# Graph network on one core: the update stage's two normalisations move from VectorE to ScalarE

## The chip, the cores and the metric

The kernel runs on one core of one Trainium2 chip. A core has TensorE (PE, with its weight loads shown as PEld), VectorE (DVE), ScalarE (ACT), GpSimd (POOL) and the queues that start transfers, SyncE's (SP) among them. The metric is the device time of one execution in microseconds; lower is better. Each engine works through its own instructions in order; semaphores connect them.

## The reference, cut to what matters

Two graph layers over 12500 nodes of 256 features and 200000 edges, each followed by a layer norm. What matters here is what is done for each node between the two edge passes:

```python
msgs = jnp.where(deg[:, None, None] > 0, agg, V)          # agg is already summed over the edges
out = msgs.reshape(N, H * D) @ Wo + bo
y = out + node_features
z = (y - mean(y)) / sqrt(var(y) + 1e-05) * gamma + beta   # end of the first layer
x1 = _layernorm(x + z)                                    # (v - m) / sqrt(var + eps)
x0_i = leaky(x1 @ W1 + b1);  x0_j = leaky(x1 @ W2 + b2)   # leaky(v) = max(v, 0.2 v)
a1 = x0_i @ wa1 + ba1[0];    a2 = x0_j @ wa2 + ba2[0]     # used by the second edge pass
```

All of it is float32.

## The kernel before

The kernel has seven stages in a row: projections of all nodes, a sort of the edges' keys beside the edge scores, the softmax, the aggregation over edges, `update_nodes` (the update stage, the node work shown above), `attend` (the second edge pass) and `finish`. Each stage is a block of its own, and the change is in `update_nodes` alone.

The nodes lie in NB = 98 blocks of 128, one node on each partition. `update_nodes` is a software pipeline written out by hand: every engine runs a loop over turns i, and in a turn it does each of its steps for the block i - lag, in the order in which the steps stand in a list. A block goes through these steps:

- DVE `divide` (lag 0) and `fill_alone` (0) make msg: the sum divided by the softmax's denominator, and V for nodes without edges. Both read two tensors in SBUF. PE `turn_msg` (0) transposes msg, ACT `copy_msg_t` (0) copies it out of PSUM, PE `project_msg` (1) multiplies by Wo.
- DVE `add_x` (2) makes y from PSUM and x. DVE `y_spread` and `y_variance` (2), ACT `root_y` (2), DVE `invert_y` (3) make mean and 1/std in columns of the tile `small`. DVE `normalise_y` (3) is line 1288: (y - mean) * (1/std), in place.
- POOL multiplies by gamma (line 1130), adds beta (1132), adds x (1134), which gives z. The first of these waits for `y_normed`.
- DVE `z_spread` and `z_variance` (5), ACT `root_z` (5), DVE `invert_z` (6), DVE `normalise_z` (6), line 1283, make x1 from z. The tiles msg, y, z and x1 have four buffers each.
- PE `turn_x1` (7) and ACT `copy_x1_t` (7) transpose x1, ACT `double` (7) writes 2 * x1 into the table of nodes, PE `project_x1` (8) multiplies by W1 and W2 at once, ACT `fifth` (8) writes 0.2 times the result, DVE `leak` (9) takes the maximum, and DVE `row_sum1` and `row_sum2` (9) make the two dot products, each with two inputs in SBUF. SP stores the rows of the block (lag 12).

In the trace the msg, y, z and x1 tiles are all called `score`, since they share that tensor's space; CUSTOM_DVE_ANT_0 is the dot product of row_sum1 (L1236) and row_sum2 (L1275), with a short reading of the accumulator behind it; BATCH_NORM_STATS2 is a spread, BATCH_NORM_AGGREGATE a variance.

DVE's order within a turn is the list in its loop: leak, add_x, z_spread, divide, row_sum1, invert_z, invert_y, y_spread, z_variance, row_sum2, normalise_z, normalise_y, y_variance, fill_alone. ACT's is fifth, copy_x1_t, root_z, double, root_y, copy_msg_t. PE's is project_x1, turn_x1, project_msg, turn_msg.

Of the kernel before, what the change touches and what calls it, by code (L numbers as in the profile page):

```python
# [7 lines left out]
ALU = mybir.AluOpType  # L8
ACT = mybir.ActivationFunctionType
# [1023 lines left out]
def update_nodes(nc, t, wo, bo, gamma, beta, w1, b1, w2, b2, wa1, ba1, wa2, ba2):  # L1033

    with ExitStack() as ctx:
# [3 lines left out]
        def ring(name, shape, n=4):  # L1039
            return [sb(f"{name}{u}", shape) for u in range(n)]  # L1040
# [4 lines left out]
        def sem(name):  # L1045
            return ctx.enter_context(nc.semaphore(name))
# [11 lines left out]
        msg, y, z, x1 = ([t["score"][:, (4 * k + u) * D:(4 * k + u + 1) * D] for u in range(4)] for k in range(4))  # L1058
        msg_t, x1_t = ring("n_msg_t", [P, 2, P]), ring("n_x1_t", [P, 2, P])
        hx, small = ring("n_hx", [P, D + XW]), ring("n_small", [P, 24], 8)  # L1060
# [7 lines left out]
        y_var, y_over, y_normed, z_stats, z_var = (sem(f"n_{n}") for n in ("y_var", "y_over", "y_normed", "z_stats", "z_var"))  # L1068
        z_over, x1_ready, a1_ready, xj_ready = (sem(f"n_{n}") for n in ("z_over", "x1_ready", "a1_ready", "xj_ready"))
        msg_t_ready, y_std, z_std, doubled, x1_t_ready, leaked = (sem(f"n_{n}") for n in ("msg_t_ready", "y_std", "z_std", "doubled", "x1_t_ready", "leaked"))  # L1070
        fifth_ready = sem("n_fifth_ready")
        msg_turned, o_ready, x1_turned, h_ready = (sem(f"n_{n}") for n in ("msg_turned", "o_ready", "x1_turned", "h_ready"))
        z_scaled, z_moved, z_ready = sem("n_z_scaled"), sem("n_z_moved"), sem("n_z_ready")
        block = ctx.enter_context(nc.Block())
# [61 lines left out]
        @block.scalar  # L1136
        def _(act):
            act.wait_ge(pads_set, 5)

            def fifth(b):  # L1140
                act.wait_ge(h_ready, b + 1)
                if b >= 4:
                    act.wait_ge(xj_ready, b - 3)
                    act.wait_ge(xj_stored[b % 4], 16 * (b // 4))
                nc.scalar.activation(hx[b % 4][:, 0:2 * D], ps_h[b % 2][:, :], ACT.Copy, scale=0.2).then_inc(fifth_ready, 1)

            def copy_x1_t(b):
                act.wait_ge(x1_turned, b + 1)
                if b >= 4:
                    act.wait_ge(h_ready, b - 3)  # L1150
                nc.scalar.copy(x1_t[b % 4][:, :, :], ps_x1[b % 2][:, :, :]).then_inc(x1_t_ready, 1)

            def root_z(b):
                act.wait_ge(z_var, b + 1)
                nc.scalar.activation(small[b % 8][:, 18:19], small[b % 8][:, 15:16], ACT.Sqrt, bias=eps[:, 0:1]).then_inc(z_std, 1)

            def double(b):
                act.wait_ge(x1_ready, b + 1)
                nc.scalar.activation(tab[:, b * AW:b * AW + D], x1[b % 4], ACT.Copy, scale=2.0).then_inc(doubled, 1)

            def root_y(b):
                act.wait_ge(y_var, b + 1)
                nc.scalar.activation(small[b % 8][:, 16:17], small[b % 8][:, 13:14], ACT.Sqrt, bias=eps[:, 0:1]).then_inc(y_std, 1)

            def copy_msg_t(b):
                act.wait_ge(msg_turned, b + 1)
                if b >= 4:
                    act.wait_ge(o_ready, b - 3)
                nc.scalar.copy(msg_t[b % 4][:, :, :], ps_msg[b % 2][:, :, :]).then_inc(msg_t_ready, 1)

            for i in range(NB + 9):
                for lag, work in ((8, fifth), (7, copy_x1_t), (5, root_z), (7, double), (2, root_y), (0, copy_msg_t)):
                    if live(i - lag):
                        work(i - lag)

# [42 lines left out]
        @block.vector  # L1218
        def _(dve):
            den = slots[:, :, D:AW]  # L1220
            dve.tensor_scalar(alone[:, :].unsqueeze(2), den[:, :, 0:1], 0.0, None, ALU.is_equal).then_inc(over_ready, 1)
            dve.tensor_scalar(over[:, :, :], den, 0.5, None, ALU.max).then_inc(over_ready, 1)
            dve.wait_ge(over_ready, 2)
            dve.reciprocal(over[:, :, :], over[:, :, :]).then_inc(over_ready, 1)
            dve.wait_ge(over_ready, 3)
            dve.wait_ge(weights_in, 12 * 16)
            dve.wait_ge(pads_set, 5)

            def leak(b):
                dve.wait_ge(fifth_ready, b + 1)  # L1230
                dve.tensor_tensor(hx[b % 4][:, 0:2 * D], ps_h[b % 2][:, :], hx[b % 4][:, 0:2 * D], ALU.max).then_inc(leaked, 1)

            def row_sum1(b):
                dve.wait_ge(leaked, b + 1)
                h = hx[b % 4]
                dve.tensor_tensor_reduce(h[:, 0:D], h[:, 0:D], wide["wa1"][:, :], 1.0, 0.0, ALU.mult, ALU.add, t["a1_tab"][:, b:b + 1])\  # L1236
                    .then_inc(a1_ready, 1)

            def add_x(b):
                dve.wait_ge(o_ready, b + 1)  # L1240
                dve.wait_ge(x_loaded[b % X_RING], 16 * (b // X_RING + 1))
                if b >= 4:
                    dve.wait_ge(z_ready, b - 3)
                dve.tensor_tensor(y[b % 4], ps_o[b % 2][:, :], x_in[b % X_RING][:, :], ALU.add).then_inc(y_ready, 1)

            def z_spread(b):
                dve.wait_ge(z_ready, b + 1)
                dve.bn_stats(small[b % 8][:, 6:12], z[b % 4]).then_inc(z_stats, 1)

            def divide(b):  # L1250
                if b >= 4:
                    dve.wait_ge(msg_turned, b - 3)
                dve.tensor_tensor(msg[b % 4].rearrange("p (h d) -> p h d", h=H), tab[:, b * AW:b * AW + D].rearrange("p (h d) -> p h d", h=H),
                                  over[:, b, :].unsqueeze(2).broadcast_to([P, H, DH]), ALU.mult).then_inc(divided, 1)

            def invert_z(b):
                dve.wait_ge(z_std, b + 1)
                dve.reciprocal(small[b % 8][:, 19:20], small[b % 8][:, 18:19]).then_inc(z_over, 1)

            def invert_y(b):  # L1260
                dve.wait_ge(y_std, b + 1)
                dve.reciprocal(small[b % 8][:, 17:18], small[b % 8][:, 16:17]).then_inc(y_over, 1)

            def y_spread(b):
                dve.wait_ge(y_ready, b + 1)
                dve.bn_stats(small[b % 8][:, 0:6], y[b % 4]).then_inc(y_stats, 1)

            def z_variance(b):
                dve.wait_ge(z_stats, b + 1)
                dve.bn_aggr(small[b % 8][:, 14:16], small[b % 8][:, 6:12]).then_inc(z_var, 1)  # L1270

            def row_sum2(b):
                dve.wait_ge(a1_ready, b + 1)
                h = hx[b % 4]
                dve.tensor_tensor_reduce(h[:, 0:D], h[:, D:2 * D], wide["wa2"][:, :], 1.0, 0.0, ALU.mult, ALU.add, h[:, 2 * D:2 * D + 1])\  # L1275
                    .then_inc(xj_ready, 1)

            def normalise_z(b):
                dve.wait_ge(z_over, b + 1)
                if b >= 4:  # L1280
                    dve.wait_ge(x1_turned, b - 3)
                    dve.wait_ge(doubled, b - 3)
                dve.tensor_scalar(x1[b % 4], z[b % 4], small[b % 8][:, 14:15], small[b % 8][:, 19:20], ALU.subtract, ALU.mult)\
                    .then_inc(x1_ready, 1)

            def normalise_y(b):
                dve.wait_ge(y_over, b + 1)
                dve.tensor_scalar(y[b % 4], y[b % 4], small[b % 8][:, 12:13], small[b % 8][:, 17:18], ALU.subtract, ALU.mult)\
                    .then_inc(y_normed, 1)

            def y_variance(b):
                dve.wait_ge(y_stats, b + 1)
                dve.bn_aggr(small[b % 8][:, 12:14], small[b % 8][:, 0:6]).then_inc(y_var, 1)

            def fill_alone(b):
                dve.wait_ge(divided, b + 1)
                dve.wait_ge(v_loaded[b % 4], 16 * (b // 4 + 1))
                dve.scalar_tensor_tensor(msg[b % 4], v_in[b % 4][:, :], alone[:, b:b + 1], msg[b % 4], ALU.mult, ALU.add).then_inc(msg_ready, 1)

            for i in range(NB + 10):  # L1300
                for lag, work in ((9, leak), (2, add_x), (5, z_spread), (0, divide), (9, row_sum1), (6, invert_z), (3, invert_y), (2, y_spread),
                                  (5, z_variance), (9, row_sum2), (6, normalise_z), (3, normalise_y), (2, y_variance), (0, fill_alone)):
                    if live(i - lag):
                        work(i - lag)
            dve.wait_ge(a1_ready, NB)
            dve.tensor_scalar(t["a1_tab"][:, :], t["a1_tab"][:, :], ba[:, 0:1], ba[:, 1:2], ALU.add, ALU.add)
            dve.wait_ge(xj_ready, NB)
# [224 lines left out]
```

## Time and profile before

| | |
|---|---|
| median of 3 runs | 7487.49 us (7469.43 to 7493.04) |
| the profiled execution | 7541.05 us, of which the span of the trace is 7539.4 |
| the update stage's full turns in it | 4561.6 to 4963.6 us after the span's start |
| busy share of the whole span | PE 71%, DVE 60%, POOL 55%, ACT 41% |

The shares of the whole span are averages over stages with different limits, so the stage itself has to be read by windows. Times in the rows are microseconds from the span's start unless marked ns. A row of the timeline gives start, length, engine, line and operation; a bracket at its end is idle time of the engine before it and what ended it.

### The profile page before, as it was taken

How to read it: one execution, taken by the hardware profiler on the slowest of the kernel's cores; microseconds unless marked ns; L12 is line 12 of the kernel's file. 1: busy time of each engine (PE TensorE's matmuls, PEld its weight loads, DVE VectorE, ACT ScalarE, POOL GpSimd, SP SyncE). 2: the span in 40 equal slices, each digit the busy share in tenths (PEclk: the TensorE clock that was granted, in tenths of full speed). 3: DMA queues.
4: the chain of work that ended last, by engine and by line, in shares of the span. 5: the costliest groups of instructions: out<-in, count | busy, mean ns of one | idle time of the engine just before them, and what ended most of it. 6: DMA issues, size and time to landing. Idle time of an engine off the chain costs nothing. (4 is left out here: it accounts for less than half of the span.)

```text
span 7539.4 us, 82733 instructions
## 1 busy us (share of the span) xinstructions
PE 5366.9 (71%) x21563; PEld 4019.8 (53%) x21563; DVE 4547.7 (60%) x8352; ACT 3080.2 (41%) x8260; POOL 4117.2 (55%) x4183
## 2 busy tenths in 40 slices
PE   5966666666667556637777768877777777777874
PEld 2445555555555444425555544446666666666663
DVE  6216666767677555578888878964444444444446
ACT  2323333333333333328777754433333333333333
POOL 1126666666667555513333325556666666666663
PEclk9976776767666676669999999987777777777776
DMA  2348888888898888816666643323333333333333
GB/s 74 106 146 281 276 292 285 276 287 289 291 299 290 287 280 275 274 36 199 199 199 199 199 142 88 88 78 92 91 91 91 91 91 91 91 91 91 91 92 112
DMA packets 857534, 1308.71 MB, mean 174 GB/s; under 512 B 87145, under 2 KB 690535, under 8 KB 856787
## 3 DMA queue, kind: packets, MB, share of 16 engines
q0 software_dynamic: 221008, 683.55, 29.1%
q1 hardware_dynamic: 629091, 613.77, 26.1%
q10 hardware_dynamic: 7010, 6.38, 0.2%
q8 instruction: 187, 3.06, 0.2%
q14 instruction: 238, 1.95, 0.1%
HBM read 1031.10 MB, written 272.26 MB: 173 GB/s over the span
## 5 line engine op out<-in xcount | busy, mean ns | idle before, releaser
L645 POOL DMA_INDIRECT s_rows<-kv_rows,other x1664 | 1737.3, 1044 | 949.3 <-issue 496.1
L1340 POOL DMA_INDIRECT t_rows<-xj_rows,other x1664 | 1626.0, 977 | 837.5 <-issue 444.6
L1415 PE MATMUL ps_xsum<-t_rows,t_hot_att 128*128 128x256 f32 x3328 | 1235.7, 536 | 417.5 <-DVE node_tab L1386 388.7
L754 PE MATMUL ps_rel<-rel,hot 64*128 64x64 f32 x3328 | 613.0, 341 | 862.6 <-DVE s_rows L737 628.5
L756 PE MATMUL ps_q<-node_tab,hot 128*128 x3328 | 1191.6, 518 | 36.1 <-issue 35.6
L1415 PEld LDWEIGHTS ps_xsum<-t_rows,t_hot_att 128*128 128x128 f32 x3328 | 863.8, 272 | 594.6 <-issue 356.1
L754 PEld LDWEIGHTS ps_rel<-rel,hot 64*128 64x128 f32 x3328 | 552.3, 249 | 1057.2 <-issue 969.3
L734 DVE TENSOR_TENSOR s_rows<-s_rows,ps_rel 128x1024 f32<-128x1024 f32 x416 | 506.4, 1217 | 931.8 <-remote 706.7
L661 ACT ACTIVATE hot<-apart,ones 128x1024 f32<-128x1024 bf16 x416 | 477.8, 1148 | 1373.3 <-remote 767.7
L1027 PE MATMUL ps_sum<-a_terms,a_hot 128*128 128x260 f32 x3328 | 830.1, 392 | 282.7 <-DVE node_tab L1006 193.3
L756 PEld LDWEIGHTS ps_q<-node_tab,hot 128*128 128x128 f32 x3328 | 817.3, 258 | 221.0 <-issue 42.6
L987 ACT ACTIVATE a_terms<-a_terms,score 128x64 f32<-128x64 f32 x3328 | 839.8, 334 | 218.8 <-DMA a_terms<-v_edges 218.1
L1386 DVE TENSOR_TENSOR node_tab<-node_tab,ps_xsum 128x256 f32 x1664 | 699.9, 421 | 363.1 <-issue 181.1
L1027 PEld LDWEIGHTS ps_sum<-a_terms,a_hot 128*128 128x128 f32 x3328 | 599.3, 190 | 513.3 <-issue 430.2
L1006 DVE TENSOR_TENSOR node_tab<-node_tab,ps_sum 128x260 f32 x1664 | 703.5, 423 | 183.0 <-DVE node_tab L1006 5.4
L972 POOL TENSOR_TENSOR a_terms<-a_terms,score 128x512 f32<-128x512 f32 x416 | 438.2, 1053 | 661.6 <-DMA a_terms<-v_edges 661.6
L1377 DVE TENSOR_TENSOR t_logit<-ps_a,t_rows 128x4 f32<-128x4 f32 x416 | 67.4, 162 | 1084.0 <-DMA x_in<-in_x 1036.4
L1360 ACT COPY t_node_hot<-ps_hot 128x512 f32<-128x512 f32 x416 | 243.8, 586 | 915.9 <-remote 831.9
L656 ACT ACTIVATE apart<-apart,minus_p 128x1024 bf16<-128x1024 bf16 x416 | 473.4, 1138 | 326.6 <-DMA apart<-what_rows 239.4
L1353 ACT ACTIVATE t_hot_att<-t_hot,t_att 128x128 f32<-128x128 f32 x1664 | 531.6, 390 | 13.6
L737 DVE TENSOR_TENSOR s_rows<-s_rows,ps_q 128x1024 f32<-128x1024 f32 x416 | 507.8, 1221 | 14.2
L739 DVE TENSOR_REDUCE score<-s_rows 128x16 f32<-128x1024 f32 x416 | 507.4, 1220 | 14.2
(208 smaller groups left out, 5835.0 us busy)
## 6 DMA issues: line engine op xcount, KB each, us to landing
v_edges<-s_rows SPq DMA_DIRECT2D x416, 512.0 KB
a_terms<-v_edges SPq DMA_DIRECT2D x416, 512.0 KB, 3.7
apart<-what_rows SPq DMA_DIRECT2D x416, 256.0 KB
s_rows<-kv_rows,other POOLq DMA_INDIRECT x1664
t_rows<-xj_rows,other POOLq DMA_INDIRECT x1664
kv_rows<-kv_out POOLq DMA_DIRECT2D x97, 256.0 KB, 2.3
xj_rows<-n_hx SPq DMA_DIRECT2D x97, 130.0 KB, 2.1
x_in<-in_x SPq DMA_DIRECT2D x97, 128.0 KB, 2.0
```

The lines of the kernel that those rows point to most:

```text
L645: pool.indirect_dma_start(out=rows[g % KV_RING][:, k, :], out_offset=None, in_=t["kv_rows"], in_offset=bass.IndirectOffsetOnAxis(ap=t["oth ...
L737: dve.tensor_tensor(key, key, ps_q[g % 2][:, :, :], ALU.mult).then_inc(picked_used, 1)
L739: dve.tensor_reduce(t["score"][:, g * U * H:(g + 1) * U * H].rearrange("p (k h) -> p k h", h=H), by_head, AX.X, ALU.add)\
L754: nc.tensor.matmul(ps_rel[g % 2][:, k, :], hot[g % 2][0:R, 1, k, :], rel_02[:, :], start=True, stop=True)
L756: last = nc.tensor.matmul(ps_q[g % 2][:, k, :], hot[g % 2][:, 0, k, :], t["node_tab"][:, bass.ds(blocks[k] * AW, D)], start=True, stop=True)
L987: last = nc.scalar.activation(head, head, ACT.Copy, scale=t["score"][:, at:at + 1])
L1006: dve.tensor_tensor(acc, acc, ps_sum[g % 2][:, k, 0:AW], ALU.add).then_inc(added, 1)
L1027: last = nc.tensor.matmul(ps_sum[g % 2][:, k, 0:AW], hot[g % 4][:, k, :], terms[g % DEEP][:, k, :], start=True, stop=True)
L1340: pool.indirect_dma_start(out=rows[g % RING][:, k, :], out_offset=None, in_=t["xj_rows"], in_offset=bass.IndirectOffsetOnAxis(ap=t["other1 ...
L1353: last = nc.scalar.activation(hot_att[g % 2][:, k, :], hot[g % 4][:, k, :], ACT.Copy, scale=att[g % 2][:, k:k + 1])
L1386: dve.tensor_tensor(acc, acc, ps_sum[g % 2][:, k, :], ALU.add).then_inc(added, 1)
L1415: last = nc.tensor.matmul(ps_sum[g % 2][:, k, :], hot_att[g % 2][:, k, :], rows[g % RING][:, k, 0:D], start=True, stop=True)
```

## The change

DVE no longer normalises. Behind each reciprocal it makes one more column, the shift -mean * (1/std): `shift_z` into column 21 of `small`, `shift_y` into column 20. ACT then computes x * (1/std) + shift with one Identity activation, which takes the scale from one column and the bias from the other: `normalise_z` (lag 6) and `normalise_y` (lag 3) stand at the end of ACT's turn. The waits of normalise_z for the buffer of x1 (`x1_turned`, `doubled`) go along with it. In DVE's turn the two reciprocals move from behind row_sum1 to behind add_x, and the shifts stand behind row_sum1. Lags, buffers and the other engines' orders stay.

```diff
# ScalarE
+            def normalise_z(b):
+                act.wait_ge(z_shift, b + 1)
+                if b >= 4:
+                    act.wait_ge(x1_turned, b - 3)
+                    act.wait_ge(doubled, b - 3)
+                nc.scalar.activation(x1[b % 4], z[b % 4], ACT.Identity, scale=small[b % 8][:, 19:20], bias=small[b % 8][:, 21:22])\
+                    .then_inc(x1_ready, 1)
+
+            def normalise_y(b):
+                act.wait_ge(y_shift, b + 1)
+                nc.scalar.activation(y[b % 4], y[b % 4], ACT.Identity, scale=small[b % 8][:, 17:18], bias=small[b % 8][:, 20:21])\
+                    .then_inc(y_normed, 1)
+
             for i in range(NB + 9):
-                for lag, work in ((8, fifth), (7, copy_x1_t), (5, root_z), (7, double), (2, root_y), (0, copy_msg_t)):
+                for lag, work in ((8, fifth), (7, copy_x1_t), (5, root_z), (7, double), (2, root_y), (0, copy_msg_t),
+                                  (6, normalise_z), (3, normalise_y)):
...
# VectorE
-            def normalise_z(b):
+            def shift_z(b):
                 dve.wait_ge(z_over, b + 1)
-                if b >= 4:
-                    dve.wait_ge(x1_turned, b - 3)
-                    dve.wait_ge(doubled, b - 3)
-                dve.tensor_scalar(x1[b % 4], z[b % 4], small[b % 8][:, 14:15], small[b % 8][:, 19:20], ALU.subtract, ALU.mult)\
-                    .then_inc(x1_ready, 1)
-
-            def normalise_y(b):
+                dve.tensor_scalar(small[b % 8][:, 21:22], small[b % 8][:, 14:15], small[b % 8][:, 19:20], -1.0, ALU.mult, ALU.mult)\
+                    .then_inc(z_shift, 1)
+
+            def shift_y(b):
                 dve.wait_ge(y_over, b + 1)
-                dve.tensor_scalar(y[b % 4], y[b % 4], small[b % 8][:, 12:13], small[b % 8][:, 17:18], ALU.subtract, ALU.mult)\
-                    .then_inc(y_normed, 1)
+                dve.tensor_scalar(small[b % 8][:, 20:21], small[b % 8][:, 12:13], small[b % 8][:, 17:18], -1.0, ALU.mult, ALU.mult)\
+                    .then_inc(y_shift, 1)
...
             for i in range(NB + 10):
-                for lag, work in ((9, leak), (2, add_x), (5, z_spread), (0, divide), (9, row_sum1), (6, invert_z), (3, invert_y), (2, y_spread),
-                                  (5, z_variance), (9, row_sum2), (6, normalise_z), (3, normalise_y), (2, y_variance), (0, fill_alone)):
+                for lag, work in ((9, leak), (2, add_x), (6, invert_z), (3, invert_y), (5, z_spread), (0, divide), (9, row_sum1), (6, shift_z),
+                                  (3, shift_y), (2, y_spread), (5, z_variance), (9, row_sum2), (2, y_variance), (0, fill_alone)):
```

## Rows read from the trace of the kernel before

**Rows 1.** Windows: stretch, its length, busy PE, PEld, DVE, ACT, POOL; clock, DMA.

```profile
4700.00:4800.00 100.00, 86.74 (x312) 41.69 (x310) 100.00 (x356) 45.08 (x136) 53.29 (x66) 1.00 0.32 88
```

**Rows 2.** Timeline, DVE: the leaks of turn 9 and turn 98.

```profile
4561.59 0.69 DVE L1231 TENSOR_TENSOR n_hx<-ps_h,n_hx 128x512 f32<-128x512 f32 x1 [1.10 <-ACT n_hx L1145]
...
4963.57 0.68 DVE L1231 TENSOR_TENSOR n_hx<-ps_h,n_hx 128x512 f32<-128x512 f32 x1
```

**Rows 3.** Timeline, DVE: one steady turn, from leak to the next leak.

```profile
4701.36 0.68 DVE L1231 TENSOR_TENSOR n_hx<-ps_h,n_hx 128x512 f32<-128x512 f32 x1
...
4701.96 0.41 DVE L1244 TENSOR_TENSOR score<-ps_o,n_x 128x256 f32<-128x256 f32 x1
...
4702.62 0.50 DVE L1253 TENSOR_TENSOR score<-node_tab,n_over 128x256 f32<-128x256 f32 x1
...
4703.04 0.94 DVE L1236 CUSTOM_DVE_ANT_0 n_hx<-n_hx,wide_wa 128x256 f32<-128x256 f32 x1
...
4703.92 0.15 DVE L1258 RECIPROCAL n_small<-n_small 128x1 f32<-128x1 f32 x1
...
4704.05 0.40 DVE L1266 BATCH_NORM_STATS2 n_small<-score 128x6 f32<-128x256 f32 x1
...
4704.46 0.39 DVE L1275 CUSTOM_DVE_ANT_0 n_hx<-n_hx,wide_wa 128x256 f32<-128x256 f32 x1
...
4704.78 0.40 DVE L1283 TENSOR_SCALAR score<-score,n_small 128x256 f32<-128x256 f32 x1
...
4705.10 0.40 DVE L1288 TENSOR_SCALAR score<-score,n_small 128x256 f32<-128x256 f32 x1
...
4705.43 0.17 DVE L1293 BATCH_NORM_AGGREGATE n_small<-n_small 128x2 f32<-128x6 f32 x1
4705.52 0.45 DVE L1298 SCALAR_TENSOR_TENSOR score<-n_v,n_alone,score 128x256 f32<-128x256 f32 x1
...
4705.89 0.68 DVE L1231 TENSOR_TENSOR n_hx<-ps_h,n_hx 128x512 f32<-128x512 f32 x1
```

**Rows 4.** Timeline, DVE: row_sum1 of turn 9.

```profile
4563.41 0.42 DVE L1236 CUSTOM_DVE_ANT_0 n_hx<-n_hx,wide_wa 128x256 f32<-128x256 f32 x1
```

**Rows 5.** Timeline, POOL: its three operations about that steady turn.

```profile
4702.11 0.74 POOL L1132 TENSOR_TENSOR score<-score,wide_beta 128x256 f32<-128x256 f32 x1
...
4702.92 0.79 POOL L1134 TENSOR_TENSOR score<-score,n_x 128x256 f32<-128x256 f32 x1
...
4705.65 0.91 POOL L1130 TENSOR_TENSOR score<-score,wide_gamma 128x256 f32<-128x256 f32 x1 [1.94 <-DVE score L1288]
```

**Rows 6.** Timeline, PE: turn_msg at both ends of a turn without waits.

```profile
4562.30 0.44 PE L1210 MATMUL ps_msg<-ident,score 128*128 128x128 f32 x2
...
4566.15 0.44 PE L1210 MATMUL ps_msg<-ident,score 128*128 128x128 f32 x2
```

**Rows 7.** Timeline, ACT: copy_msg_t, fifth and copy_x1_t of the steady turn.

```profile
4701.97 0.37 ACT L1169 COPY n_msg_t<-ps_msg 128x256 f32<-128x256 f32 x1 [0.57 <-PE ps_msg L1210]
...
4704.00 0.60 ACT L1145 ACTIVATE n_hx<-ps_h 128x512 f32<-128x512 f32 x1 [1.66 <-PE ps_h L1187]
...
4704.50 0.37 ACT L1151 COPY n_x_t<-ps_x 128x256 f32<-128x256 f32 x1
```

**Rows 8.** Groups of ACT, whole span: busy us, mean ns, idle before.

```profile
L1353 ACT ACTIVATE t_hot_att<-t_hot,t_att 128x128 f32<-128x128 f32 x1664 | 531.6, 390 | 13.6
L310 ACT ACTIVATE enh<-ps_xt,q 128x128 f32<-128x128 f32 x196 | 61.8, 376 | 7.4 <-PE ps_xt L339 7.4
...
L1159 ACT ACTIVATE node_tab<-score 128x256 f32<-128x256 f32 x98 | 40.6, 415 | 0.0
...
L1163 ACT ACT_TABLE_LOAD x1 | 1.3, 1283 | 0.0
```

**Rows 9.** Line L371 (ns min/median/max), and POOL's timeline beside it.

```profile
L371 DVE TENSOR_SCALAR pbit<-pid x7: 153/154/154, 72.1 to 73.2; 128x1 int32<-128x1 int32 x7
...
72.28 0.42 POOL L102 TENSOR_TENSOR b_rest<-b_qkv,b_part 6x128 f32<-6x128 f32 x1
```

More of the change, by code:

```diff
@@ L1070, in update_nodes @@
         msg_t_ready, y_std, z_std, doubled, x1_t_ready, leaked = (sem(f"n_{n}") for n in ("msg_t_ready", "y_std", "z_std", "doubled", "x1_t_ready", "leaked"))
-        fifth_ready = sem("n_fifth_ready")
+        fifth_ready, y_shift, z_shift = sem("n_fifth_ready"), sem("n_y_shift"), sem("n_z_shift")
         msg_turned, o_ready, x1_turned, h_ready = (sem(f"n_{n}") for n in ("msg_turned", "o_ready", "x1_turned", "h_ready"))
```

## The prediction, made before the changed kernel was run

> **What bounds the kernel now.** I read the windows by stage first. From turn 9 of the update stage on, DVE is busy for all 100.00 us of a 100 us window, PE for 86.74 at full clock, ACT for 45.08, POOL for 53.29 [rows 1]. So in the full turns the stage runs at DVE's pace: whatever leaves DVE's queue shortens the turn, until another engine takes over. Next I read the timeline for the two leaks that bound the 89 full turns (block 97's last DVE work included): (4963.57 - 4561.59) / 89 = 4.517 us a turn [rows 2]. Then one turn of DVE, start by start [rows 3]. The reader is to see in it that the displayed lengths overlap by about 0.08 us (fill_alone ends at 4705.97, leak starts at 4705.89), so that a cost is the distance between starts; and that one operation is out of line. row_sum1 lasts 0.94 us; the same operation took 0.42 in turn 9, when POOL was idle [rows 4]. In the steady turn it starts at 4703.04, while POOL's last addition runs from 4702.92 to 4703.71 [rows 5]. Likewise `divide` takes 0.50 beside POOL's second operation. The pairs fit an exclusive hold: a DVE operation that reads two tensors in SBUF waits until about 0.14 us before the end of a POOL operation that started first (4703.98 - 0.42 = 4703.56 beside an end at 4703.71; 4703.12 less the 0.41 that add_x takes for the same shape = 4702.71, beside an end at 4702.85), and a POOL operation that meets a DVE one is stretched: 0.91 in place of the 0.74 of the second, so that it gets its inputs as if it had asked for them 0.14 to 0.15 after its start (4705.97 - 4705.65 - 0.17) [rows 3, 5]. leak and add_x have one input in PSUM and stand beside POOL unharmed. So where POOL's three operations lie in DVE's turn is worth 0.6 us now, and the change moves them.
>
> **The edit, DVE.** Out go the two 128x256 normalisations: y_variance starts 0.65 us after normalise_z [rows 3]. In come two products on one column, shift_z and shift_y. The nearest row is `reciprocal` on a column, 0.15 long, with 0.13 for the pair start to start [rows 3]; a 128x1 TENSOR_SCALAR with constants is 0.154 long [rows 9]. A scalar read from SBUF may add as much as a column costs, so the pair lies between 0.13 and 0.26; I take 0.26, the dearer end, since both read a column as their scalar. Moving the reciprocals changes no sum. Free of POOL, the turn is 4.53 - 0.65 + 0.26 - 0.52 (row_sum1) - 0.09 (divide) = 3.53.
>
> **ACT** gets two 128x256 passes. Nothing here has scale and bias columns together. Below: L1159's plain pass, 0.415 [rows 8]. With a scale column, 128 columns of L1353 take 0.390; the slope between 512 and 256 columns, (0.60 - 0.37) / 256, adds 0.115: 0.50 [rows 7, 8]. L310's bias column costs 0.12 over 0.37 - 0.115, which gives at most 0.62. Start to start is 0.10 less (L1145 is 0.60 long, its successor starts after 0.50 [rows 7]): 0.32, 0.40, 0.52. I take 0.40 to 0.52; ACT's busy time then goes from 2.04 us a turn (0.4508 x 4.52) to 2.9 to 3.1, so it isn't the bound, and its old duties are ahead of the passes in its queue.
>
> **Where the passes lie decides.** normalise_z and normalise_y stand behind copy_msg_t, which waits for fill_alone and PE's transposes of the same turn. With F the end of fill_alone as zero, copy_msg_t starts at 0.53 (4701.97 against 4701.44) [rows 3, 7], the passes at 0.80 and 1.20 to 1.32, the second ends at 1.70 to 1.94, and POOL starts 0.15 later, as it does behind normalise_y today (4705.10 + 0.40, 4705.65) [rows 3, 5]: p = 1.85 to 2.09. Today it starts 0.32 before F. What waits for it, z_spread, comes two turns later; what waits for x1_ready (at 1.42 at the latest) is turn_x1, which PE reaches only behind project_x1, whose end starts fifth at 4704.00, 2.56 after F [rows 7]. Both are covered. PE's queue is not reordered, nor SP's; SP waits for z_ready only six blocks back and for msg_ready four.
>
> **The new turn**, with the distances of [rows 3] (add_x and z_spread are 0.66 together, y_spread to row_sum2 is 0.41), from F: leak -0.08, add_x 0.52, invert_z 0.85, invert_y 0.92, z_spread 0.98, divide 1.31 (no POOL beside it now), row_sum1 1.64, that is before p. It ends at 2.06; POOL's first operation is stretched to max(p, 1.92) + 0.73 = 2.65 to 2.82. DVE: shift_z 1.98, shift_y 2.11, y_spread 2.24, row_sum2 at 2.65 (0.41 on), held up by 0 to 0.03, ends 3.04. POOL's second wants to start at 2.73 to 2.90 and is held by row_sum2, ends at 3.04 - 0.14 + 0.73 = 3.63. y_variance 2.97, fill_alone 3.06: it meets POOL's second, gets the inputs at 3.49, ends at **3.94 to 3.98; I take 3.95**. So the 0.6 of waiting for POOL doesn't vanish: it moves from row_sum1 to fill_alone and is 0.43 there. POOL's third ends about 0.6 after F, clear of divide.
>
> **PE's floor.** Between 4562.30 and 4566.15 PE waited for nothing: 3.85 us a turn [rows 6]. So PE is nearly the bound; P can't be under 3.85 in full turns.
>
> **Sum.** 89 x (4.517 - 3.95) = 50.5 us. In the nine turns ahead of these DVE waits for the others (1.10 us before turn 9's leak [rows 2]), and in the nine behind them project_x1 and the work behind it remain; y_normed half a turn later costs them nothing, or up to the 2 us by which it is late; I take 0. Against the profiled execution (7539.4 us of span, 7541.05 in all) that is 7490.5; on the median of the runs, 7487.49, which is 0.7% below it, 7437. The stage ran at full clock in the profile and the edit touches no other, so the difference carries over in us, not in per cent.
>
> [...] In the rows of a steady turn no TENSOR_SCALAR meets POOL. Seven on one column, back to back from 72.1 to 73.2, all took 153 to 154 ns, though POOL ran a TENSOR_TENSOR from 72.28 to 72.70 among them [rows 9]: a column isn't held up. [...]
>
> **Rivals.** Faster by over 0.3% means over 22.5 us, or 0.25 us a turn; within that a measurement can't tell it from no change.
> (a) The shifts are held by POOL's first operation, which waits behind row_sum1 and goes ahead of them: shift_z at 2.51 instead of 1.98, row_sum2 then 3.18, held by POOL's second (which waited for shift_y) to 3.31, fill_alone 3.72 held by the third to 4.15, F at 4.60. 89 x 0.08 = +8: 7495. [...] Against it: the 153 ns rows. 7 in 100.
> (b) POOL comes first: p below 1.64, so that row_sum1 waits as it does today. It needs ACT's passes at the plain 0.415 (p = 0.80 + 0.32 + 0.42 + 0.15 = 1.69) and 0.05 more. Then row_sum1 gets its inputs at 2.2, row_sum2 runs 3.19 to 3.58, POOL's third is held by it and ends at 4.17, fill_alone waits to 4.03: F at 4.49, 7485, no change. The margin is small, but both column rows say the passes are dearer. 8 in 100.
> (c) Slower: the table of ACT's functions. A table load is 1.28 us [rows 8]. If Identity and Sqrt didn't share one, every turn would have two loads: ACT's starts sum to about 2.5 + 2.57 = 5.07 us, 89 x 0.55 = +49: 7536. It decides from 2.0 us more on ACT in a turn; one load would not. Against it: Copy and Sqrt already alternate under the single load of L1163, and Identity and Copy under the first one. 3 in 100.
> (d) An undrawn wait (POOL later than 2.1, or a lost slot of ACT) puts the turn at 4.1 to 4.4: 7450 to 7477. For it: p is the least certain of my terms, and from p = 2.05 on every 0.1 costs 0.1. 13 in 100, most of it still faster by over 0.3%.
>
> **Numbers.** My forecast, P from 3.85 to 4.05, has 68 in 100: 7428 to 7446, and with the spread of the runs 7422 to 7455. For 8 in 10 I add (d) and most of (b): 7422 to 7485. Faster: 0.68 and 0.10 of (d), 0.78. Same: (a), (b), the rest of (d), 0.18. Slower: (c) and what I have not thought of, 0.04.
>
> **What would show it.** After: full turns of 3.95 us; PE over 0.95 busy; row_sum1 near 0.42 and fill_alone near 0.88; POOL's first operation starting 1.85 to 2.09 after fill_alone's end, ended by ACT; no column shift over 0.25 us; ACT passes of 0.50 to 0.62; one table load in the stage. Wrong if row_sum1 is still 0.9 long (b), if the shifts are 0.5 long (a), if table loads stand in the turns (c).

## The result and the profile after

The changed kernel takes 7440.25 us in the median of 6 runs (7426.93 to 7447.64) against 7487.02 for the kernel before, also 6 runs: a ratio of 0.9936, with a 95% interval from 0.9924 to 0.9947. The forecast was 7437 in a range of 7422 to 7485.

The windows of the changed kernel, with the columns of [rows 1]:

```profile
4700.00:4800.00 100.00, 100.00 (x358) 48.08 (x357) 100.00 (x412) 74.06 (x205) 58.50 (x77) 1.00 0.38 102
```

In [rows 1] only DVE was busy throughout. Now PE's row shows 100.00 as well (its ends are modelled, so waits of 0.1 us vanish in it), ACT's share rose from 45 to 74, and the clock stayed at full. The two leaks that bound the 89 full turns, from the timeline:

```profile
4531.33 0.69 DVE L1245 TENSOR_TENSOR n_hx<-ps_h,n_hx 128x512 f32<-128x512 f32 x1 [1.30 <-ACT n_hx L1145]
...
4879.69 0.68 DVE L1245 TENSOR_TENSOR n_hx<-ps_h,n_hx 128x512 f32<-128x512 f32 x1
```

That is (4879.69 - 4531.33) / 89 = 3.914 us a turn against 4.517 in [rows 2], so 53.6 us less in the full turns. Turn 9, the first of them, took 4.48 us (4.13 before); the other 88 took 3.908 on average, against 4.521. The rest of the stage kept its length: from the first divide to the first leak 34.4 us (33.9 before), from leak 98 to the last row_sum2 27.6 (27.6). The span fell by more, 7539.4 to 7444.0, but 31 of those us lie ahead of the stage and 11 behind it, where nothing was edited. The profiled execution of the kernel before, 7541.05 us, lies outside its six runs (7469.43 to 7498.27), so these two spans can't be set against each other. That is why the stage is read by itself and the whole by medians.

One turn of the timeline answers to [rows 3], [rows 5] and [rows 7]. It begins with fill_alone, whose end, 4703.09 + 0.85 = 4703.94, is the zero of the prediction's positions:

```profile
4703.09 0.85 DVE L1309 SCALAR_TENSOR_TENSOR score<-n_v,n_alone,score 128x256 f32<-128x256 f32 x1
...
4704.46 0.37 ACT L1169 COPY n_msg_t<-ps_msg 128x256 f32<-128x256 f32 x1 [0.33 <-PE ps_msg L1224]
...
4704.73 0.60 ACT L1176 ACTIVATE score<-score,n_small 128x256 f32<-128x256 f32 x1
...
4705.23 0.59 ACT L1181 ACTIVATE score<-score,n_small 128x256 f32<-128x256 f32 x1
4705.24 0.40 DVE L1267 TENSOR_TENSOR score<-node_tab,n_over 128x256 f32<-128x256 f32 x1
...
4705.57 0.41 DVE L1250 CUSTOM_DVE_ANT_0 n_hx<-n_hx,wide_wa 128x256 f32<-128x256 f32 x1
...
4705.91 0.20 DVE L1294 TENSOR_SCALAR n_small<-n_small 128x1 f32<-128x1 f32 x1
4705.97 0.72 POOL L1130 TENSOR_TENSOR score<-score,wide_gamma 128x256 f32<-128x256 f32 x1 [1.45 <-ACT score L1181]
4706.04 0.20 DVE L1299 TENSOR_SCALAR n_small<-n_small 128x1 f32<-128x1 f32 x1
...
4706.57 0.40 DVE L1289 CUSTOM_DVE_ANT_0 n_hx<-n_hx,wide_wa 128x256 f32<-128x256 f32 x1
4706.77 0.79 POOL L1132 TENSOR_TENSOR score<-score,wide_beta 128x256 f32<-128x256 f32 x1
...
4707.00 0.84 DVE L1309 SCALAR_TENSOR_TENSOR score<-n_v,n_alone,score 128x256 f32<-128x256 f32 x1
```

The reader is to see four things. The second pass ends at 4705.82 and POOL starts 2.03 us after fill_alone's end, released by ACT (in [rows 5] by DVE, 0.32 before it). row_sum1 is 0.41 long, not 0.94. fill_alone is 0.84 long, not 0.45: it starts at 4707.00, inside POOL's second operation (4706.77 to 4707.56). And shift_y runs from 4706.04 to 4706.24 beside POOL's first operation without a stretch of either.

### The profile page after: what moved, and what is told of

The parts are those of the page before. It is cut to its first block and busy times, and to the rows that moved or that the text cites. A ratio compares the mean times of both kernels' runs of the same rounds, so it can differ in the third digit from the quotient of the medians.

```text
span 7444.0 us, 82929 instructions
## 1 busy us (share of the span) xinstructions
PE 5245.8 (70%) x21563; PEld 3935.2 (53%) x21563; DVE 4486.9 (60%) x8352; ACT 3169.2 (43%) x8456; POOL 4088.2 (55%) x4183
## 3 DMA queue, kind: packets, MB, share of 16 engines
q8 instruction: 187, 3.06, 0.2%
q14 instruction: 240, 1.97, 0.1%
## 5 line engine op out<-in xcount | busy, mean ns | idle before, releaser
L1426 PE MATMUL ps_xsum<-t_rows,t_hot_att 128*128 128x256 f32 x3328 | 1184.7, 519 | 484.3 <-DVE node_tab L1397 449.1
L756 PE MATMUL ps_q<-node_tab,hot 128*128 x3328 | 1168.3, 509 | 53.1 <-issue 52.4
L754 PE MATMUL ps_rel<-rel,hot 64*128 64x64 f32 x3328 | 597.9, 335 | 855.4 <-DVE s_rows L737 615.5
L1426 PEld LDWEIGHTS ps_xsum<-t_rows,t_hot_att 128*128 128x128 f32 x3328 | 832.3, 262 | 648.2 <-issue 439.3
L756 PEld LDWEIGHTS ps_q<-node_tab,hot 128*128 128x128 f32 x3328 | 800.8, 252 | 234.9 <-issue 64.9
```

The lines of the kernel that those rows point to most:

```text
L754: nc.tensor.matmul(ps_rel[g % 2][:, k, :], hot[g % 2][0:R, 1, k, :], rel_02[:, :], start=True, stop=True)
L756: last = nc.tensor.matmul(ps_q[g % 2][:, k, :], hot[g % 2][:, 0, k, :], t["node_tab"][:, bass.ds(blocks[k] * AW, D)], start=True, stop=True)
L1426: last = nc.tensor.matmul(ps_sum[g % 2][:, k, :], hot_att[g % 2][:, k, :], rows[g % RING][:, k, 0:D], start=True, stop=True)
```

## The experiments

Two theories go through all of them. **Queue:** only what leaves or enters DVE's queue counts, since DVE is the bound. **Holding:** a DVE operation with two inputs in SBUF, or a 256-column TENSOR_SCALAR, and a POOL operation shut each other out, the first to start going first, so that the positions of both count. The second part rests on normalise_z in y_only, below. The turn of each kernel is read as above, from two leaks 89 turns apart:

| kernel | leaks of turn 9 and turn 98 | full turn, us | expected (holding) | median, us | ratio, 95% interval |
|---|---|---|---|---|---|
| before | 4561.59, 4963.57 | 4.517 | | 7487.02 | 1 |
| changed | 4531.33, 4879.69 | 3.914 | 3.95 | 7440.25 | 0.9936 (0.9924 to 0.9947) |
| order_only | 4552.27, 4942.91 | 4.389 | 4.43 | 7532.67 | 0.9992 (0.9982 to 1.0002) |
| passes_old_order | 4547.20, 4895.81 | 3.917 | 3.91 | 7485.90 | 0.9927 (0.9911 to 0.9944) |
| y_only | 4542.02, 4956.99 | 4.663 | 4.57 to 4.75 | 7552.26 | 1.0018 (1.0006 to 1.0029) |
| z_only | 4557.97, 4960.61 | 4.524 | 4.49 | 7541.72 | 1.0005 (0.9995 to 1.0015) |
| passes_before_copy | 4527.86, 4925.87 | 4.472 | 4.04 | 7484.29 | 0.9995 (0.9983 to 1.0007) |
| y_after_fifth | 4512.26, 4857.82 | 3.883 | 3.85 | 7432.74 | 0.9933 (0.9918 to 0.9948) |
| before_no_beta | 4527.75, 4883.21 | 3.994 | 3.98 | 7452.85 (one run) | |
| after_no_beta | 4522.55, 4871.23 | 3.918 | 3.91 | 7433.23 (one run) | |
| after_again | 4072.65, 4421.01 | 3.914 | 3.91 | 6632.60 | 0.9928 (0.9914 to 0.9941) |
| four_apart | 4071.51, 4414.51 | 3.854 | 3.85 | 6628.96 | 0.9916 (0.9902 to 0.9930) |
| four_apart_no_b12 | 4077.03, 4401.44 | 3.645 | 3.65 | 6610.05 (one run) | |

The groups ran on three different chips, so a median is only to be set against the kernel before of its own group: 7536.75 us for the first four experiments, 7487.18 for the next four, 6683.89 for the last three. The ratios do that.

**order_only: the order alone.**

```diff
-(9, leak), (2, add_x), (5, z_spread), (0, divide), (9, row_sum1), (6, invert_z), (3, invert_y), (2, y_spread), ...
+(9, leak), (2, add_x), (6, invert_z), (3, invert_y), (5, z_spread), (0, divide), (9, row_sum1), (2, y_spread), ...
```

> The kernel before with only invert_z and invert_y moved from behind row_sum1 to behind add_x. Two theories. Holding: a DVE operation with two SBUF inputs waits for a POOL operation that started first, so the place of each against POOL's three counts. Divide then starts 1.31 us after fill_alone's end instead of 1.18, when POOL's second operation has let go (about 1.27), and is no longer held (0.41 long, not 0.49); row_sum1 still is (about 0.95). Full turn 4.43 us against 4.52, so 8 us less: about 7479. Queue: only what leaves or enters DVE's queue counts, so 4.52 and no change.

Most turns are 4.43 us long; nine of 4.03 bring the mean to 4.389. DVE's queue has the same operations in it, so the 0.09 of a typical turn came from where divide lies. By the line's own rows, min/median/max in ns:

```profile
L1253 DVE TENSOR_TENSOR score<-node_tab,n_over x98: 395/401/930, 4518.5 to 4939.9; 128x256 f32<-128x256 f32 x98
...
L1236 DVE CUSTOM_DVE_ANT_0 n_hx<-n_hx,wide_wa x98: 399/942/947, 4554.2 to 4970.1; 128x256 f32<-128x256 f32 x98
```

divide's median fell from 0.49 to 0.40, row_sum1's is still 0.94. The 11 us that the stage lost are at the edge of what the whole-kernel ratio can tell (0.9982 to 1.0002).

The turns of 4.03 were not expected. In them row_sum1 went ahead of POOL's third operation, which had started 0.17 before it, and in the next turn POOL went first with the same lead:

```profile
4633.32 1.16 POOL L1134 TENSOR_TENSOR score<-score,n_x 128x256 f32<-128x256 f32 x1
4633.49 0.41 DVE L1236 CUSTOM_DVE_ANT_0 n_hx<-n_hx,wide_wa 128x256 f32<-128x256 f32 x1
...
4637.35 0.82 POOL L1134 TENSOR_TENSOR score<-score,n_x 128x256 f32<-128x256 f32 x1
4637.52 0.94 DVE L1236 CUSTOM_DVE_ANT_0 n_hx<-n_hx,wide_wa 128x256 f32<-128x256 f32 x1
```

So the first to start does not always go first.

**passes_old_order: the move alone.**

```diff
-... (2, add_x), (6, invert_z), (3, invert_y), (5, z_spread), (0, divide), (9, row_sum1), (6, shift_z), (3, shift_y), (2, y_spread), (5, z_variance), (9, row_sum2), ...
+... (2, add_x), (5, z_spread), (0, divide), (9, row_sum1), (6, invert_z), (3, invert_y), (2, y_spread), (5, z_variance), (9, row_sum2), (6, shift_z), (3, shift_y), ...
```

> Both passes on ACT as in the changed kernel, but DVE's order as before (reciprocals behind row_sum1, shifts where the normalisations were). Holding: row_sum1 starts 1.51 after fill_alone's end and is free, row_sum2 comes to 2.39, inside POOL's first operation (2.03 to 2.76), waits until about 2.61; fill_alone then gets its inputs at about 3.46: full turn 3.91 us, as in the changed kernel (3.91 measured), with the waiting split between row_sum2 (0.62 long) and fill_alone (about 0.63). The new order is worth nothing: 7440. A theory that gives the order a share of the gain expects 4.0 or more.

```profile
L1289 DVE CUSTOM_DVE_ANT_0 n_hx<-n_hx,wide_wa x98: 389/644/916, 4550.0 to 4923.5; 128x256 f32<-128x256 f32 x98
...
L1309 DVE SCALAR_TENSOR_TENSOR score<-n_v,n_alone,score x98: 452/601/740, 4513.8 to 4895.3; 128x256 f32<-128x256 f32 x98
```

The waiting is split as expected, 0.24 at row_sum2 and 0.16 at fill_alone instead of 0.40 at fill_alone, and the turn is the same. With both passes on ACT, the new order is worth nothing.

**y_only and z_only: one pass each.** The other normalisation goes back to DVE, in the place of its shift.

```diff
# y_only, DVE: normalise_z as before, in the place of shift_z; ACT:
-                                  (6, normalise_z), (3, normalise_y)):
+                                  (3, normalise_y)):
# z_only, DVE: normalise_y as before, in the place of shift_y; ACT:
-                                  (6, normalise_z), (3, normalise_y)):
+                                  (6, normalise_z)):
```

> Only normalise_y on ACT; normalise_z stays on DVE, in the place of shift_z. Queue: about half of the gain, a turn of 4.1 to 4.2 us, 7460. Holding: without normalise_z ahead of it, normalise_y ends 0.5 us earlier and POOL starts 1.54 after fill_alone's end instead of 2.03, beside row_sum1 (1.64). Then normalise_z is held by POOL's first operation (0.8 long, as its longest in the trace of before), row_sum2 by the second a little, fill_alone by the third: full turn 4.57 us, up to 4.75. So no gain at all: 7492, 7487 to 7508.

> Only normalise_z on ACT; normalise_y stays on DVE, in the place of shift_y. Queue: a turn of 4.1 to 4.2 us, 7460. Holding: POOL starts 0.15 after normalise_y, 2.66 after fill_alone's end, and row_sum2 starts at 2.84: if POOL's operation goes first, row_sum2 is held to 3.22 and fill_alone by the second to 4.05, a turn of 4.49 us and 7485; if row_sum2 goes first, 4.11 us and 7451. A DVE start 0.13 behind POOL's was held in the trace of before, so I take 4.49.

One pass taken off DVE's full queue gains nothing: y_only is slightly slower than the kernel before (interval 1.0006 to 1.0029), z_only can't be told from it. Both together gain 53.6 us. That is the sharpest cut between the theories; the queue theory expected 4.1 to 4.2 for each. The timeline of y_only shows what happens to normalise_z:

```profile
4702.26 1.09 POOL L1130 TENSOR_TENSOR score<-score,wide_gamma 128x256 f32<-128x256 f32 x1 [2.29 <-ACT score L1181]
4702.35 0.41 DVE L1250 CUSTOM_DVE_ANT_0 n_hx<-n_hx,wide_wa 128x256 f32<-128x256 f32 x1
...
4702.69 0.81 DVE L1297 TENSOR_SCALAR score<-score,n_small 128x256 f32<-128x256 f32 x1
```

Here row_sum1 went ahead of POOL, POOL's first operation (1.09 long) waited for it, and normalise_z (0.81 in place of 0.40) waited for POOL. In the next turn POOL went first and row_sum1 was 0.94 long:

```profile
4706.84 0.76 POOL L1130 TENSOR_TENSOR score<-score,wide_gamma 128x256 f32<-128x256 f32 x1 [1.82 <-ACT score L1181]
4706.94 0.94 DVE L1250 CUSTOM_DVE_ANT_0 n_hx<-n_hx,wide_wa 128x256 f32<-128x256 f32 x1
```

The two orders mostly alternate, with turns of 4.59 and 4.72 us. In z_only it is row_sum2, 0.19 behind POOL's start, and again fill_alone:

```profile
4705.63 0.73 POOL L1130 TENSOR_TENSOR score<-score,wide_gamma 128x256 f32<-128x256 f32 x1 [2.06 <-DVE score L1299]
...
4705.82 0.81 DVE L1289 CUSTOM_DVE_ANT_0 n_hx<-n_hx,wide_wa 128x256 f32<-128x256 f32 x1
```

**passes_before_copy: ACT's order alone.**

```diff
-(8, fifth), (7, copy_x1_t), (5, root_z), (7, double), (2, root_y), (0, copy_msg_t), (6, normalise_z), (3, normalise_y)
+(8, fifth), (7, copy_x1_t), (5, root_z), (7, double), (2, root_y), (6, normalise_z), (3, normalise_y), (0, copy_msg_t)
```

> The changed kernel with ACT's two passes ahead of copy_msg_t instead of behind it. ACT does the same work and is not the bound (74 us of 100). Queue: no change, 3.91 us a turn. Holding: normalise_y now ends 5.10 us after the fill_alone of the turn before, so POOL starts at 5.25 less the turn's length after the new one, about 1.2, ahead of row_sum1 (1.64), which it holds to about 1.78; the second lets row_sum2 pass, the third holds fill_alone. Turn and start are tied (a longer turn starts POOL earlier), which settles near 4.04 us, 12 us more: 7452. The shifts, which now lie under POOL's operations, stay 0.20 long if a one-column TENSOR_SCALAR isn't held, and become up to 0.7 if it is.

The direction was right, the size was not: 4.472 us a turn, so that nearly the whole gain is gone by swapping three entries in the list of an engine that is 74% busy. Turns 10 and 11 took 3.90 and 3.89, the next two 4.44 and 4.32, and from then on they stayed at 4.49. The timeline of two turns at the point where it tips, and of a late one:

```profile
4537.59 1.00 POOL L1130 TENSOR_TENSOR score<-score,wide_gamma 128x256 f32<-128x256 f32 x1 [1.04 <-ACT score L1181]
4537.59 0.41 DVE L1250 CUSTOM_DVE_ANT_0 n_hx<-n_hx,wide_wa 128x256 f32<-128x256 f32 x1
...
4541.44 0.72 POOL L1130 TENSOR_TENSOR score<-score,wide_gamma 128x256 f32<-128x256 f32 x1 [1.00 <-ACT score L1181]
4541.48 0.95 DVE L1250 CUSTOM_DVE_ANT_0 n_hx<-n_hx,wide_wa 128x256 f32<-128x256 f32 x1
...
4702.52 0.73 POOL L1130 TENSOR_TENSOR score<-score,wide_gamma 128x256 f32<-128x256 f32 x1 [2.03 <-ACT score L1181]
4702.67 0.87 DVE L1267 TENSOR_TENSOR score<-node_tab,n_over 128x256 f32<-128x256 f32 x1
4703.33 0.79 POOL L1132 TENSOR_TENSOR score<-score,wide_beta 128x256 f32<-128x256 f32 x1
4703.46 0.94 DVE L1250 CUSTOM_DVE_ANT_0 n_hx<-n_hx,wide_wa 128x256 f32<-128x256 f32 x1
...
4705.41 0.45 DVE L1309 SCALAR_TENSOR_TENSOR score<-n_v,n_alone,score 128x256 f32<-128x256 f32 x1
```

What I left out of the expectation: a start near 1.2 us after fill_alone's end lies ahead of divide (1.31) too. Once POOL comes first, divide is held for 0.46 and row_sum1 for 0.53, while fill_alone no longer waits its 0.40 (0.45 long). The turn is longer by the difference, 0.59 (4.49 against 3.91). By the argument of the expectation a longer turn starts POOL still earlier against it, so that the state would hold itself; that is argued and fits the 4.49 that stayed, but no run tests it alone. The shifts stayed at 0.20 under POOL's third operation, 0.213 at the longest of 98.

**before_no_beta and after_no_beta: less work on POOL.** z is y times gamma plus x in both; beta is left out.

```diff
-                nc.gpsimd.tensor_tensor(z[b % 4], z[b % 4], wide["beta"][:, :], ALU.add).then_inc(z_moved, 1)
-                pool.wait_ge(z_moved, b + 1)
```

> The kernel before without POOL's addition of beta (z is then y times gamma plus x), so that POOL has two operations a turn and DVE's work is untouched. Holding: POOL is through 1.40 us after fill_alone's end, row_sum1 (1.6) is no longer held (0.42, not 0.94), divide is held by up to 0.1: full turn 3.98 us against 4.52, about 48 us less. Queue: POOL isn't the bound (53 of 100 us busy), so 4.52.

> The changed kernel without POOL's addition of beta. Holding: POOL's second operation, now the addition of x, lies where the addition of beta was and holds fill_alone just the same: 3.91 us a turn, no change. If what counts is how much POOL works, not where, the turn falls to PE's 3.85 and fill_alone to about 0.45.

```profile
L1234 DVE CUSTOM_DVE_ANT_0 n_hx<-n_hx,wide_wa x98: 410/412/827, 4529.6 to 4910.4; 128x256 f32<-128x256 f32 x98
```

```profile
L1307 DVE SCALAR_TENSOR_TENSOR score<-n_v,n_alone,score x98: 465/843/848, 4489.1 to 4870.5; 128x256 f32<-128x256 f32 x98
```

The first is row_sum1 of before_no_beta: 0.412 for 0.941. One POOL operation less, with DVE's queue untouched, takes 0.52 us off each turn of the kernel before, 46.5 us in all, nearly as much as the change does. (The one run of the whole kernel lies 34 us under the median of its group.) The second is fill_alone of after_no_beta, 0.843 as in the changed kernel, and the turn is the same 3.92. So it isn't how much POOL does but what lies beside what.

**y_after_fifth: POOL and DVE's two-input operations apart.**

```diff
# ACT
-(8, fifth), (7, copy_x1_t), (5, root_z), (7, double), (2, root_y), (0, copy_msg_t), (6, normalise_z), (3, normalise_y)
+(8, fifth), (3, normalise_y), (7, copy_x1_t), (5, root_z), (7, double), (2, root_y), (0, copy_msg_t), (6, normalise_z)
# DVE
+(9, leak), (2, add_x), (6, invert_z), (3, invert_y), (5, z_spread), (6, shift_z), (3, shift_y), (2, y_spread),
+(5, z_variance), (2, y_variance), (9, row_sum1), (9, row_sum2), (0, divide), (0, fill_alone)
```

> A version that keeps POOL and DVE's two-input operations apart: normalise_y directly behind fifth in ACT's turn (POOL then starts at fill_alone's end, 3.80 us after the one before), and row_sum1, row_sum2, divide, fill_alone as the last four of DVE's turn, behind all operations with one SBUF input. Holding: DVE's turn would be about 3.67 us with 0.16 of waiting, so PE becomes the bound at its 3.85: 5 us less than the changed kernel, 7435, fill_alone 0.45 long and DVE idle for 0.1 to 0.2 a turn. Queue: 3.91, no change. If PE's floor of 3.85 isn't one, the turn falls to 3.7.

fill_alone's median is 0.485, so its waiting for POOL is gone, but the turn is 3.883, not 3.85. The timeline shows two gaps that I hadn't drawn:

```profile
4704.94 0.47 DVE L1250 CUSTOM_DVE_ANT_0 n_hx<-n_hx,wide_wa 128x256 f32<-128x256 f32 x1
...
4705.45 0.42 DVE L1289 CUSTOM_DVE_ANT_0 n_hx<-n_hx,wide_wa 128x256 f32<-128x256 f32 x1
...
4705.80 0.42 DVE L1267 TENSOR_TENSOR score<-node_tab,n_over 128x256 f32<-128x256 f32 x1
...
4706.26 0.48 DVE L1309 SCALAR_TENSOR_TENSOR score<-n_v,n_alone,score 128x256 f32<-128x256 f32 x1
```

fill_alone starts 0.46 behind divide, whose result it waits for, where divide starts 0.35 behind row_sum2, for which it doesn't wait. row_sum2, which waits for row_sum1, starts 0.51 behind it; 0.06 of that is row_sum1's own length (0.47 in place of 0.41). The next version sets something between each such pair.

**four_apart, beside the changed kernel, and without the biases of W1 and W2.** The last of the three leaves b1 and b2 out of the result. The first diff is against y_after_fifth, whose order of ACT it keeps, the second against four_apart.

```diff
# four_apart, DVE
-(5, z_variance), (2, y_variance), (9, row_sum1), (9, row_sum2), (0, divide), (0, fill_alone)
+(5, z_variance), (9, row_sum1), (2, y_variance), (0, divide), (9, row_sum2), (0, fill_alone)
# four_apart_no_b12, PE: the stop moves to the second matmul
-                nc.tensor.matmul(ps_h[b % 2][:, :], ones_h[0:3, :], b_parts[:, D:3 * D], start=False, stop=True).then_inc(h_ready, 1)
```

> The changed kernel unedited, as the measure on this chip for the two versions beside it: full turn 3.91 us, 0.9936 of the kernel before within its interval (0.992 to 0.995).

> y_after_fifth with the end of DVE's turn set anew: row_sum1, y_variance, divide, row_sum2, fill_alone in place of y_variance, row_sum1, row_sum2, divide, fill_alone. In y_after_fifth row_sum2 started 0.46 after row_sum1 and fill_alone 0.46 after divide, each being the one right behind the result that it waits for, where the same pairs with another operation between took 0.34 and 0.33. Theory: DVE's 3.88 us a turn there was set by these two waits of 0.12; with an operation in each, DVE comes to about 3.65 and PE's 3.85 is the bound. About 3 us less than y_after_fifth, 5 less than the changed kernel, in the stage; too little for the ratio, to be read from the turn. Rival: DVE's queue isn't what made 3.88 (semaphore steps between PE and DVE), then it stays 3.88.

> four_apart without the matmul that adds b1 and b2 (they are left out of the result), 0.31 us of PE's turn. If PE's queue is the bound of four_apart, its turn falls from 3.85 to that of DVE, about 3.65; if something else holds it there, it stays 3.85.

The windows, first of four_apart, then of four_apart_no_b12:

```profile
4200.00:4300.00 100.00, 100.00 (x365) 48.90 (x364) 100.00 (x417) 72.41 (x209) 56.70 (x78) 1.00 0.39 104
```

```profile
4200.00:4300.00 100.00, 94.78 (x361) 51.70 (x360) 100.00 (x440) 77.02 (x221) 60.15 (x83) 1.00 0.42 110
```

four_apart is at 3.854, and after turn 9 (4.30) its turns are 3.83 to 3.87, 3.849 on average: PE's 3.85 from [rows 6]. Without one matmul the turn falls to 3.645, so PE's queue was the bound, and PE's share falls below 100. In four_apart row_sum1 is 0.73 long (it comes while POOL's third operation runs), in the one without the matmul 0.53: DVE still meets POOL where it runs ahead of PE, at no cost. The 0.060 us less a turn are 5.4 us in 89 turns; turns 100 and 101 are 3.74 long instead of 3.25, and with the two before them that gives back about 1.2. In the medians it is 3.6 us (6628.96 against 6632.60), within the spread, and the two intervals overlap. By the trace this version is the faster one; by the medians that isn't shown.

## Why the prediction was right

Point by point, by its own steps:

- **The bound.** DVE in the full turns: right, though turn 9 took 4.48 and not 3.95, with row_sum2 0.74 long and fill_alone 0.84; the rest of the stage kept its length to within 0.5 us, where I took 0.
- **DVE's edit.** 0.65 out. The two shifts, of which I took the dearer bound of 0.26, take 4705.91 to 4706.16 (y_spread starts 0.25 after shift_z): right. A column read as the scalar costs about 0.05 of length (0.20 against the 0.154 of [rows 9]).
- **ACT's passes.** 0.60 and 0.59 long, the distance between them 0.50; range 0.50 to 0.62 and 0.40 to 0.52, at the upper end, so with both columns each costs its own.
- **POOL's start.** 2.03 after fill_alone's end, in the range of 1.85 to 2.09, and behind row_sum1 (1.63).
- **The new turn.** Drawn 3.94 to 3.98, measured 3.914. shift_z 1.97 (1.98), row_sum2 2.63 (2.65), its end 3.03 (3.04), POOL's second to 3.62 (3.63), fill_alone at 3.06 (3.06) and its end at 3.90 (3.94). The 0.04 is the end: fill_alone's inputs came about 0.17 before POOL's shown end, where I had 0.14, and its wait was 0.40, not 0.43. In the 88 turns behind turn 9 the forecast was 88 x 0.042 = 3.7 us too long, in turn 9 0.5 too short: 3 us in all.
- **The sum.** 50.5 us forecast, 53.6 in the full turns of the profile, 46.8 between the medians (interval of the ratio: 40 to 57 us). That the forecast of 7437 lies 3 us beside the median is within the spread of the runs (7426.93 to 7447.64) and says less than the turn does. That the difference carries over in us, not in per cent, is supported by the stage, whose 89 turns take 348.36 us in both profiles of the changed kernel, though one lies in a run of 7445.70 us and the other in one of 6632.60 (the kernel before was profiled in neither place). The medians can't tell: where the kernel before takes 6684 us the change saved 51.3, its interval is 39 to 57, and the same share as here would be 42.
- **Rival (a), shifts held:** no. shift_y lies beside POOL's first operation at 0.20, the longest of 98 was 0.208, and in passes_before_copy both lay under POOL's operations. The row of [rows 9] was the right guide. The Trainium skill, Vector Engine (DVE) Microarchitecture Reference, section Performance modes, lets a TENSOR_SCALAR use both read ports where the outermost dimension that is not of length one is even, or odd and as long in the output. A single column has no such dimension, so the rule as written gives no reason for a wait, and the trace shows none. For 256 columns there was one: normalise_z took 0.81 beside POOL in y_only. The Trainium skill, SBUF — State Buffer, section Who interferes with whom, says that a tensor_scalar in a two-port mode and GpSimd shut each other out, whoever issues first going first. The 0.81 agrees with the first half, though the trace doesn't show which mode it ran in; order_only shows that the starts in the trace don't always tell who goes first.
- **Rival (b), POOL first:** not in the changed kernel, where the margin turned out to be 0.4 us. passes_before_copy shows that the mechanism is real: 4.47 us a turn, near the rival's 4.49, though there divide and row_sum1 are the ones held, not row_sum1 and fill_alone.
- **Rival (c), table loads:** one load in the stage, as before.
- **Rival (d), an undrawn wait:** none.

The argument for the forecast was stronger than for "0.65 us leave DVE's queue": by that alone y_only and z_only should each have gained over 25 us, and neither did. The same positions, laid out for other orders ahead of the runs, gave the turn within 0.04 us in eight of the ten edited kernels, and within its range of 4.57 to 4.75 in y_only. The exception, passes_before_copy, had a position left out, not a wrong cost. There was luck in two of the eight: z_only and order_only rest on POOL going first in a near tie, and in nine turns of order_only it didn't.

## What to carry to other kernels

Where DVE is the bound and POOL works beside it, lay both out against each other before counting what an edit takes off DVE: half an edit can gain nothing, and swapping entries in the list of an engine that has room can take the whole gain back, because it decides when POOL starts. Put DVE's operations with one SBUF input beside POOL's (but not a TENSOR_SCALAR of 256 columns, which was held in y_only), and the ones with two together where POOL is idle; between an operation and the one that reads its result set a third. Then look at the next engine's turn without waits: here PE's 3.85 left 0.06 us to gain by perfect order, out of 0.40 of waiting that looked like much.

## What the runs showed of the hardware that I had not expected

- Which side goes first when both start close together is not clean. In passes_before_copy POOL's start 0.04 us ahead of row_sum1 (4541.44, 4541.48) won and an equal one (4537.59) lost. In y_only one 0.09 ahead lost (4702.26, 4702.35) while one 0.10 ahead won a turn later (4706.84, 4706.94). In order_only a lead of 0.17 lost once (4633.32, 4633.49) and won in the next turn (4637.35, 4637.52); of the leads of 0.15 to 0.17 there, 78 won and 9 lost. In z_only all of 0.19 to 0.20 won. So a layout in which POOL starts up to 0.17 us ahead of a DVE operation can't be relied on. What decides was not tried; in the lost cases of order_only and y_only shown here another two-input operation of DVE, divide, was still running when POOL started, but so it was in the won ones.
- The stages around this one can run far faster without an edit, this one did not. The kernel before took 7487, 7537 and 6684 us in three groups of runs. The changed kernel's 89 turns take 348.36 us in both of its profiles, one with a median of 7440.25, one of 6632.60; the update stage starts 4497 us into the span of the first and 4037 into that of the second, and the mean granted clock over the span is 0.792 and 0.833. Whether that is the chip, and why the stages ahead of it and behind it are faster there, was not tried.
